# First feed-forward stage of a fused four-layer block: order of the expert groups, engine of the key blocks, place of the activation-table loads

## What is computed

```python
x = x + tanh(g_xattn[0]) * L0_xattn(layernorm(x), ctx, ctx)
x = x + tanh(g_ffn[0]) * L0_ffn(layernorm(x))      # the stage that changes
x = x + tanh(g_xattn[1]) * L1_xattn(layernorm(x), ctx)   # its keys come from ctx alone
...
def L0_ffn(x):                                     # 16 experts of width 64, one shared of width 352
    shared = silu(x @ shared_gate.T) * (x @ shared_up.T) @ shared_down.T
    shared = shared * sigmoid(x @ shared_gate_w.T)
    logits = x @ gate_w.T
    rw, sel = top_k(softmax(logits), 2)            # normalised to sum 1
    combine = scatter(rw at sel)                   # N x 16
    h = silu(x @ w_gate) * (x @ w_up)              # per expert
    return einsum('nef,efd,ne->nd', h, w_down, combine) + shared
```

## Time and profile before

| | |
|---|---|
| median of 3 runs | 1601.91 us (1597.54 to 1604.3) |
| the profiled execution | 1598.2 us, of that 1596.4 us span |
| TensorE matmul busy | 1356.1 us, 85% |
| VectorE busy | 1086.4 us, 68% |
| ScalarE busy | 746.2 us, 47% |
| GpSimd busy | 362.1 us, 23% |
| chain that ended last | TensorE 58%, VectorE 24%, ScalarE 7%, issue 6%, GpSimd 2% |
| mean granted TensorE clock | 0.964 of full speed |

### The profile page before, as it was taken

How to read it: one execution, slowest core, us unless ns; L and a number is a source line. 1 busy time by engine, 2 the same in 40 slices (tenths; PEclk the granted TensorE clock), 3 DMA queues, 4 the chain that set the end, 5 groups by cost and what they waited for, 6 DMA issues and landing times.

```text
span 1596.4 us, 28486 instructions
## 1 busy us (share of the span) xinstructions
PE 1356.1 (85%) x10940; PEld 896.8 (56%) x10940; DVE 1086.4 (68%) x3253; ACT 746.2 (47%) x1406; POOL 362.1 (23%) x302
## 2 busy tenths in 40 slices
PE   4788987897987998798898899889788799888977
PEld 4455744564654664466465575446556467445745
DVE  3456975877656796686764687687755669658774
ACT  0144544763334643575324553467433455257632
POOL 1131310540131220251014031054013212015300
PEclk8799999999999999999899999999999999899999
DMA  9000000000000000000000000000000000000000
GB/s 355 2 1 1 1 1 1 1 1 17 1 7 1 1 1 1 1 1 16 3 1 7 1 1 1 1 1 2 17 1 7 1 1 1 1 1 2 1 1 7
DMA packets 15094, 18.95 MB, mean 12 GB/s; under 512 B 2776, under 2 KB 13672, under 8 KB 14444
## 3 DMA queue, kind: packets, MB, share of 16 engines
q1 hardware_dynamic: 14960, 17.13, 3.1%
HBM read 16.08 MB, written 1.05 MB: 11 GB/s over the span
## 4 chain that ended last, share of the span: by engine, by line
PE 58%; DVE 24%; ACT 7%; issue 6%; POOL 2%; DVEq 0%; POOLq 0%; ACTq 0%
PE bank L1034 7%; PE bank L1045 5%; PE bank L1422 4%; PE bank L1427 4%; PE bank L846 3%; PE bank L1263 3%; DVE work L640 2%; DVE small L646 2%; PE bank L1833 2%; PE bank L1815 2%; PE bank L870 2%; PE bank L1415 2%; DVE small L639 2%; PE bank L1458 2%; PE bank L347 2%
## 5 line engine op out<-in xcount | busy, mean ns | idle before, releaser
L267 POOL TENSOR_TENSOR root<-variance,minus_half 128x2 f32<-128x2 f32 (+1 forms) x72 | 55.3, 768 | 691.5 <-DVE variance L284 421.1
L1087 ACT ACTIVATE work<-bank,w_f 128x512 f32<-128x512 f32 x128 | 88.0, 688 | 90.4 <-PE bank L1034 90.1
L1045 PEld LDWEIGHTS bank<-w_f1d,work 128*128 128x128 f32 x1024 | 119.1, 192 | 13.4 <-issue 13.4
L1045 PE MATMUL bank<-w_f1d,work 128*128 128x129 f32 x1024 | 119.9, 275 | 0.0
L1034 PE MATMUL bank<-xnT,w_f 128*128 128x512 f32 x256 | 118.5, 608 | 0.0
L1596 ACT ACTIVATE work<-work,small 128x128 f32<-128x128 f32 x256 | 78.5, 390 | 84.8 <-DVE small L1723 84.8
L1654 POOL TENSOR_TENSOR small<-small 128x16 f32<-128x16 f32 x32 | 92.9, 2904 | 106.5 <-DVE small L1682 104.9
L639 DVE TENSOR_REDUCE small<-bank 128x8 f32<-128x512 f32 x96 | 65.6, 684 | 32.6 <-PE bank L506 32.6
L1681 DVE TENSOR_REDUCE small<-work 128x16 f32<-128x1024 f32 x48 | 58.4, 1217 | 40.3 <-ACT work L1560 38.7
L521 PE MATMUL bank<-consts,work 128*128 128x128 f32 x384 | 58.9, 291 | 27.9 <-ACT work L605 27.3
L1422 PE MATMUL bank<-w_x,cxT 128*128 128x512 f32 x128 | 62.3, 608 | 21.9 <-DVE work L1695 17.1
(11 more groups left out here) (284 smaller groups left out, 3211.5 us busy)
## 6 DMA issues: line engine op xcount, KB each, us to landing
w_f<-in_f_dram SPq DMA_DIRECT2D x1, 2616.0 KB
w_f<-in_f_dram SPq DMA_DIRECT2D x1, 2180.0 KB, 26.5
w_x<-in_x_dram SPq DMA_DIRECT2D x1, 2115.0 KB
w_l<-in_l_dram SPq DMA_DIRECT2D x1, 2088.5 KB, 20.7
w_f1d<-in_f1d_dram SPq DMA_DIRECT2D x4, 512.0 KB
work<-in_x_dram SPq DMA_DIRECT2D x4, 256.0 KB, 2.9
work<-in_ctx_dram SPq DMA_DIRECT2D x4, 256.0 KB, 3.3
out_dram<-x SPq DMA_DIRECT2D x4, 256.0 KB, 2.3
```

The source lines that it names most:

```text
L1045: pe.matmul(z_of(e, t)[:, 0:129], hT[e % 2][:, c, t * P:(t + 1) * P], w_f1d[:, c, e, :], start=(c == 0), stop=(c == 3))
L1087: act.activation(hT[e % 2][:, c, :], banks[n % 3][:, :], ACT.Relu, bias=k_f1["b1"][:, n:n + 1]).then_inc(hT_ready, 1)
```

## The change

- `ffn0` walks the steps in a new order: (0, 4), (1, 4), then the routed groups of tiles 0 and 1, then tiles 2 and 3 as before. Sums over groups now start and end with the first and last step of a tile.
- VectorE computes `sig`, then the first gate, and only then the routing weights. Two multiplications by 0.5 go: one into the Tanh's scale, and the differences are made right behind the two best.
- `key_blocks` moves from GpSimd (shared steps) to VectorE, behind the gates of steps 6, 8, 10 and 15.
- `load_table`, a one-column activation, brings the table load to the start of `ffn0` (Silu), to its end (Exp) and to the start of `ffn3` (Gelu).
- GpSimd's memset of `h_shared` goes to VectorE, ahead of the wait for the router.

```diff
+        def load_table(act, function):
+
+            act.activation(small[:, 960:961], ones[:, 0:1], function)
...
-            steps = [(t, g) for t in range(TILES) for g in range(5)]
+            SHARED = 4
+            steps = [(0, SHARED), (1, SHARED)] + [(t, g) for t in (0, 1) for g in range(4)]
+            steps += [(t, g) for t in (2, 3) for g in range(5)]
+            first_step = {t: min(s for s in range(len(steps)) if steps[s][0] == t) for t in range(TILES)}
+            last_step = {t: max(s for s in range(len(steps)) if steps[s][0] == t) for t in range(TILES)}
+            tile_ended = {s: t for t, s in last_step.items()}
+            KEYS_BEHIND = (6, 8, 10, 15)
...
                     def down(s):
-                        if g == 0 and t >= 2:
+                        if s == first_step[t] and t >= 2:
                             pe.wait_ge(taken, due(taken, t - 1))
-                        if s == 0:
-                            pe.wait_ge(comb_ready, due(comb_ready, 1))
...
                 def _(act):
+                    load_table(act, ACT.Silu)
                     take_pairs(act, turn_no)
                     act.wait_ge(halves_ready, due(halves_ready, 1))
-                    act.activation(sig, halves, ACT.Tanh).then_inc(sig_ready, 1)
+                    act.activation(sig, halves, ACT.Tanh, scale=0.5).then_inc(sig_ready, 1)
...
                             take_T(s - 1)
+                    load_table(act, ACT.Exp)
...
                     pool.wait_ge(comb_ready, due(comb_ready, 1))
-                    pool.memset(h_shared[:, :, 352:384], 0.0)
...
-                        else:
-                            kv1.key_blocks(pool, t)
-                        if (t, g) == (0, 1) and i > 0:
+                        if (t, g) == (0, 0) and i > 0:
                             give_root(pool, 4)
...
+                    link(dve.memset(h_shared[:, :, 352:384], 0.0))
                     dve.wait_ge(routed, due(routed, 1))
...
+                    def differences(best):
+                        link.last_of([dve.tensor_tensor(halves[:, :, 0:1], best[:, :, 0:1], best[:, :, 1:2], ALU.subtract),
+                                      dve.tensor_copy(halves[:, :, 1:2], logits[:, :, 16:17])])
+                        dve.sem_inc(halves_ready, 1)
+
+                    best, place = top_two(dve, link, lg, 16, 160, with_best=differences)
...
+                    dve.wait_ge(sig_ready, due(sig_ready, 1))
+                    link(dve.tensor_scalar(sig, sig, 0.5, 0.5, ALU.mult, ALU.add))
+                    gate_up(0)
+                    link(dve.tensor_scalar(rest, sig[:, :, 0:1], -1.0, 1.0, ALU.mult, ALU.add))
+                    spread(dve, link, comb, tmp, place, sig[:, :, 0:1], rest, 16)
+                    dve.sem_inc(comb_ready, 1)
...
-                    for s in range(n + 2):
+                    for s in range(1, n + 2):
                         if s < n:
                             gate_up(s)
...
-                        if s >= 2 and steps[s - 2][1] == 4:
-                            t = steps[s - 2][0]
+                        if s in KEYS_BEHIND:
+                            dve.wait_ge(kv1.k_ready, due(kv1.k_ready, 1))
+                            kv1.key_blocks(dve, KEYS_BEHIND.index(s))
+                        if s - 2 in tile_ended:
+                            t = tile_ended[s - 2]
...
                 def _(act):
+                    load_table(act, ACT.Gelu)
                     take_pairs(act, turn_no)
```

More of the change, by code:

```diff
@@ L822, in h_of @@
                 def h_of(s):
-                    return h_shared[:, (s // 5) % 2, :] if steps[s][1] == 4 else hid[s % 2]
+                    return h_shared[:, steps[s][0] % 2, :] if steps[s][1] == 4 else hid[s % 2]
                 @block.tensor
@@ L871, in down @@
                                           k_l0["down"][:, (2 * g + c) * D:(2 * g + c + 1) * D],
-                                          start=(g == 0 and c == 0), stop=(g == 4 and c == 2))
+                                          start=(s == first_step[t] and c == 0), stop=(s == last_step[t] and c == n - 1))
                         m.then_inc(down_done, 1)
@@ L935, in _ @@
                     link(dve.tensor_copy(lg, logits[:, :, 0:16]))
-                    best, place = top_two(dve, link, lg, 16, 160)
-                    link(dve.tensor_tensor(halves[:, :, 0:1], best[:, :, 0:1], best[:, :, 1:2], ALU.subtract))
-                    link(dve.tensor_scalar(halves[:, :, 0:1], halves[:, :, 0:1], 0.5, None, ALU.mult))
-                    dve.tensor_scalar(halves[:, :, 1:2], logits[:, :, 16:17], 0.5, None,
-                                      ALU.mult).then_inc(halves_ready, 1)
-                    dve.wait_ge(sig_ready, due(sig_ready, 1))
-                    link(dve.tensor_scalar(sig, sig, 0.5, 0.5, ALU.mult, ALU.add))
-                    link(dve.tensor_scalar(rest, sig[:, :, 0:1], -1.0, 1.0, ALU.mult, ALU.add))
-                    spread(dve, link, comb, tmp, place, sig[:, :, 0:1], rest, 16)
-                    dve.sem_inc(comb_ready, 1)
+                    def differences(best):
[3 more added lines that the diff above has]
+                    best, place = top_two(dve, link, lg, 16, 160, with_best=differences)
                     def gate_up(s):
```

## The result

The changed kernel takes 1580.84 us (median of 4 runs, 1570.64 to 1586.25), the one before 1600.07 us in the runs beside it: ratio **0.9864**, 95% interval 0.9837 to 0.989. The profiled execution took 1580.86 us, its span is 1579.1 against 1596.4 us. Forecast were 1588.9 us, within 1578 to 1598.

The account below looks back on a forecast made before the run. In the routed loop GpSimd, VectorE and TensorE were taken as almost equally long per step, with large waits at the start. Block gains of 4.5, 3.0, 2.3 and 3.1, together 12.9, say 13 us, gave 1588.9 us; range 1578 to 1598.

Parts of the forecast that it names:

- the first rival: Key blocks hide: GpSimd gets its reads in between VectorE's products, 9 us come back, gain near 22 us, 1580; chance 0.2.
- Start: Start of block 1's `ffn0`: TensorE idles 0.8 instead of 3.94 us ahead of the first `turn`, gain 3.1.
- Clock at the start: Behind block 1's first wait: the short wait no longer lowers the clock; 5.5 us at 0.52 give back 2.6.
- GpSimd's key blocks: Late in block 1's stage: TensorE's idle times of 0.69 and 1.24 beside GpSimd's key blocks go, gain 1.9.
- Last norm: VectorE's last norm, blocks 1 to 3: root 0.45, L337 0.1, L340 0.25, store 0.45 too soon; cost 1.25.
- VectorE's key blocks: Products beside GpSimd's weightings in `ffn0`: each gate 0.75 late, cost 0.67 each, four in a block, 2.7.
- The room of 0.08: Routed loop of `ffn0`: any delay of a gate beyond 0.08 us reaches TensorE.
- Loads: Moved table loads: cost 0.3 x 3 and 0.3 x 4 at `ffn0`'s start and end; Exp gains 0.8 x 4, Gelu 0.6 x 4.
- the rival of dearer loads: Seven exposed loads each hold the copy behind for 1.28 us again: 9 us go, gain 4, 1597.9; chance 0.05.
- The clock falls somewhere else: Rival: the stage may lose its 6.6 us of clock gain again; gain 6.4, 1595.5; chance 0.15.
- VectorE as the bound: Rival at each key block: VectorE becomes the bound, a block costs 2.0 instead of 0.67; slower by 8, 1610; chance 0.04.
- the sign: Whether the change gains or loses: it turns at 1.48 us for a key block, almost one whole step.

Follow-up runs that it names:

- the halves: Changed kernel with each VectorE key block cut into two 128x512 halves, behind steps 6, 8, 9, 10, 15, 17, 18 and 19: 1575.87 us, ratio 0.9844.
- The late gate: Changed kernel with the first step's gate times up put behind VectorE's routing weights again: 1580.82 us, ratio 0.9882 against the kernel before.

## Why the prediction was right, point by point

The measured 1580.84 us lie within the range, 8 us below the forecast and close to the 1580 of the first rival, which did not happen as told. The start and GpSimd's side went as forecast, one term was priced at about twice what it cost, one step was not in the sum, and what the stage gained beyond the forecast was partly lost elsewhere. Of the forecast, 3.4 us in block 1 belonged to the stage as cut here (4.5 less the 1.4 of Exp and Gelu, without the 0.3 taken off at L377), 8.2 in the four; 5.60 and 18.85 came.

- **Start, right.** Idle 0.73 where 0.8 was walked, `turn(0)` 0.73 us behind the second shared `up`. Loads and key blocks without the new order have idle 3.29, all together 0.73.
- **Clock at the start, right for this place.** The granted clock went from 0.52 to 1.00. In block 2 I had expected the shared `up` at the lower level; they ran at the full one, and the stage was 40.92. That it is the short wait that keeps the clock up is only partly shown. For it: in block 1 the kernels with idle 0.73 or 1.64 have 1.00, and in those that wait 2.09 or more with the `up` at full clock it falls within the wait or 0.4 us behind it. Against it: with the order alone (blocks 1 and 2), and in block 2 with the halves and with the key blocks on GpSimd (mean 0.96 each), the clock was low ahead of the wait.
- **GpSimd's key blocks, right.** L340 0.74, L292 at most 0.35, the late waits of the earlier trace rows gone.
- **Last norm, right in the loop, wrong at the store.** By starts the `turn` behind the root is 0.58 late, behind L337 0.13 and behind L340 0.10: 0.81 where 0.8 was walked (0.45, 0.1 and 0.25). The 0.45 for the store did not come: the first key block starts at 456.48, as its gate ends (456.02 + 0.42).
- **VectorE's key blocks, the term that was mis-sized**: "the gate comes 0.75 late, cost 0.67 … four in a block, 2.7". Each stretched weighting is as described (1.22 instead of 0.61), but in block 1 the four took 1.22, 0.67, 1.21 and 1.14, and by starts TensorE's `turn` came 0.53, 0, 0.53 and 0.23 late: 1.3, not 2.7. The room of 0.08 was read rightly; two other things were not. I had 0.89 of the weighting beside the product and 0.74 of it lost; there were 0.75 beside it (456.96 to 457.71) and 0.61 lost, and 0.61 less 0.08 is the 0.53. And I had priced each product alone: where TensorE is already 0.53 late, the next `silu` is late too, and the next weighting starts 1.02 us into its product (460.59, the product at 459.57), meets only its last 0.20 and costs nothing. Moved to the end of the stage the key blocks free 1.26, 0.89 and 0.94 us, with one of the four still costing 0.56, which fits 1.3 to 1.4 in a block; 0.38 of block 1's 1.26 belong to the step of the next point. The rival that they hide was right by half: 1.3 of the 2.7 came back, though the weightings beside a product did not keep their 0.61. By the Trainium skill (SBUF — State Buffer, SBUF: two separate sides) the engine that starts second waits for the whole instruction of the first. The trace agrees but for 0.14 of the 0.75 us; with halves of 0.69 the loss is 0.08.
- **A step that the sum did not have.** In each block one weighting stands behind the root that GpSimd makes for the next stage (L267). Its `turn` was 0.87 late by starts before; it is 0.63, 0.28, 0.27 in blocks 1 to 3 and 0.25 in block 0 now, 2.0 us gained in the four. With the key blocks alone it is 0.58, so a part of the gain came with them; the rest no run separates. `down` and `turn` of block 2, before and then after:

```profile
857.42 0.60 PE L870 MATMUL bank<-w_l,work 128*128 128x128 f32 x4
858.73 0.44 PE L857 MATMUL bank<-consts,work 128*128 128x128 f32 x2 [0.70 <-DVE work L956]
...
849.36 0.60 PE L878 MATMUL bank<-w_l,work 128*128 128x128 f32 x4
850.08 0.44 PE L867 MATMUL bank<-consts,work 128*128 128x128 f32 x2
```
- **Loads.** Exp: attention 1 at full clock 25.97 instead of 26.94, 0.97 for the 0.8 priced. Gelu less the load at L377: `ffn3` 37.83 instead of 38.19 in blocks 1 and 2 (0.36 for 0.3). That the load of block 0 costs nothing, which the sum had taken without saying so, was wrong by 0.5 us: the queue stands at a barrier. Nothing was added behind a load, as the row had shown (480.59 + 1.28, the next activation at 481.89); the rival of dearer loads falls.
- **The clock falls somewhere else, half right.** The stage won back its low clock, but the rest lost about 5 us: it should have gained 5.0 by Exp and Gelu (4 x 0.97 + 3 x 0.36), lost 0.5 in block 0 and 1.4 to a preparation that ended later (61.57 against 60.14 at the first transposes), and got 1.55 longer instead. The chance of 0.15 was for a clock that falls in this stage; it fell outside.
- **VectorE as the bound, wrong way.** No key block cost a step; the sign never came near.

Of the signs that were named, three came out otherwise: the stages took 40.9 to 41.3 us, not 42 to 44; the stretched weightings 1.14 to 1.22, not 1.3 to 1.4; and stages behind `ffn0` did get longer by more than a microsecond (`ffn1` of block 1 by 2.14, all outside the stage by 1.55 in sum), which had been named as a sign of being wrong. For `ffn1` the rows above show the lower clock beside it.

So 10.7 us too little was forecast in the four stages, of that about 5 for the key blocks (4 x 1.3), 1.35 for the store (3 x 0.45), 2.0 for the step behind the root, 1.0 for block 2's shared `up`, and the rest in small terms; outside it was 6.3 too much (4.7 gained, against 1.55 lost). The errors partly cancelled: that the total fell well within the range is in part luck.

What stays open: why the low clock takes less time in one kernel than in another. The late gate shows it best, 7.2 us lost in the stage and none in the total.

## What to carry to other kernels

Give the first product after a router something that needs no routing weights, and only then move the table load: here the load alone moved the wait by 0.1 us, the order alone by 2.2, the whole change by 3.2. Cut an operation of VectorE that runs beside GpSimd's short ones so that it ends before they start, or put it where nobody waits for them. Read a delay of TensorE from start to start: the shown waits of 0.36 stood for 0.53. Judge a change of a few microseconds by the length of its stage at the same granted clock, since the total can hide 7 us.

## What the runs showed of the hardware that I had not expected

- A GpSimd multiplication of 256 columns takes 0.61 us alone, 1.22 beside a VectorE product of 1.22 that began 0.48 earlier, and 0.69 beside one of 0.69. It loses what both share, less 0.14: 0.61 of 0.75, 0.06 of 0.20, 0.08 of 0.22.
- The same code, executed again, has stretches at the lower clock in other places; single executions of the changed kernel had spans from 1568.8 us (mean clock 0.970) to 1586.6 (0.959), while a stage at full clock repeats within 0.01 us.
- The lower clock costs nothing where TensorE would have waited: with the order alone, 43.83 us in block 1 at a mean of 0.96, 43.80 in block 3 at 1.00.
- A kernel that saves time in one place can have a lower mean clock: 0.956 (12 executions) with the loads alone, which shorten attention 1 of block 1 by 0.95 us, and 0.960 (55) before. That the one causes the other is not shown.
